# Moving the softmax reciprocals and their products at the end of a graph attention layer

## The reference, cut to what matters

```python
hl = x @ Wl.T + bl
hr = x @ Wr.T + br
s = (jnp.take(hl, src, axis=0) + jnp.take(hr, dst, axis=0)) * alpha   # alpha: edge_attr_128
s = jnp.where(s >= 0, s, SLOPE * s)                                   # leaky ReLU
smax = jax.ops.segment_max(s, dst, num_segments=n_nodes)
e = jnp.exp(s - jnp.take(smax, dst, axis=0))
denom = jax.ops.segment_sum(e, dst, num_segments=n_nodes)
att = e / jnp.take(denom, dst, axis=0)
msg = jnp.take(x, src, axis=0) * att
agg = jax.ops.segment_sum(msg, dst, num_segments=n_nodes)
out = _layernorm(x + agg, axis=-1)
```

## Time and profile before

| | |
|---|---|
| median of three runs | 1168.29 us |
| profiled execution | 1168.55 us |
| its span | 1166.5 us |
| VectorE busy | 1081.4 us (93%) |
| TensorE busy (matmul) | 1083.9 us (93%) |
| ScalarE busy | 950.3 us (81%) |
| GpSimd busy | 853.4 us (73%) |
| share of GpSimd in the chain that ended last | 55% |

### The profile page before, as it was taken

The page is one execution under the profiler, slowest core; times in us unless marked ns, Lnnn a source line. Parts: engine busy times, 40 slices in busy tenths (PEclk is TensorE's granted clock), DMA queues, the critical chain, the costliest instruction groups (busy, mean ns, idle before and its releaser), DMA issues.

```text
span 1166.5 us, 35708 instructions
## 1 busy us (share of the span) xinstructions
PE 1083.9 (93%) x9359; PEld 903.1 (77%) x9359; DVE 1081.4 (93%) x1466; ACT 950.3 (81%) x2396; POOL 853.4 (73%) x879
## 2 busy tenths in 40 slices
PE   5779999999999999999999999999999999999885
PEld 5648888888788878787887888787877878878763
DVE  6549999999999999999999999999999999999988
ACT  2548888888888888888888888888888888888895
POOL 6477777777777777777777777777777777777772
PEclk9889999999999999999999999999999999999998
DMA  8676666666666666666766666666666666666623
GB/s 221 226 218 194 187 187 189 182 193 189 180 187 185 187 183 187 185 185 186 187 184 181 186 186 184 184 186 178 187 181 183 186 188 184 184 187 185 173 64 110
DMA packets 220971, 213.49 MB, mean 183 GB/s; under 512 B 32765, under 2 KB 193796, under 8 KB 220682
## 3 DMA queue, kind: packets, MB, share of 16 engines
q0 software_dynamic: 40320, 109.96, 33.9%
q1 hardware_dynamic: 180005, 100.86, 31.2%
q10 hardware_dynamic: 461, 0.40, 0.1%
HBM read 200.39 MB, written 11.47 MB: 182 GB/s over the span
## 4 chain that ended last, share of the span: by engine, by line
POOL 55%; issue 19%; PE 15%; DVE 4%; DMA 3%; ACT 2%; SPq 1%; ACTq 0%; DVEq 0%; POOLq 0%
POOL xg L389 54%; PE ps_w L580 5%; PE ps_u L545 3%; PE ps_u L549 2%; PE ps_sT L538 2%; PE ps_z L567 1%; DVE acc L891 1%; DVE stats L962 1%; PE ps_q L561 1%; PE ps_q L589 1%; POOL attr L372 1%; DMA acc<-x_in 1%; DMA attr<-chunk_rows,chunk_at 1%; DMA line<-step_lines 1%; SPq L269 1%
## 5 line engine op out<-in xcount | busy, mean ns | idle before, releaser
L389 POOL DMA_INDIRECT xg<-gather_rows,srcT x832 | 798.8, 960 | 266.8 <-issue 252.1
L580 PE MATMUL ps_w<-onehot,ex 128*128 128x128 f32 x3328 | 407.5, 276 | 3.6 <-ACT acc L708 2.5
L580 PEld LDWEIGHTS ps_w<-onehot,ex 128*128 128x128 f32 x3328 | 389.6, 193 | 4.3 <-issue 4.3
L901 DVE TENSOR_TENSOR_SCAN ps_F<-line,B,ps_sT 128x512 f32<-128x512 bf16 x208 | 266.0, 1279 | 2.0 <-DMA line<-step_lines 1.0
L549 PEld LDWEIGHTS ps_u<-right,onehotT 128*128 128x128 bf16 x2496 | 161.8, 98 | 122.5 <-issue 120.5
L912 DVE TENSOR_TENSOR_SCAN B<-line,ps_F 128x512 f32<-128x512 bf16 x208 | 251.1, 1207 | 0.0
L545 PE MATMUL ps_u<-xg,ident 128*128 128x512 f32 x416 | 219.7, 610 | 26.8 <-DMA xg<-gather_rows,srcT 21.6
L672 ACT ACTIVATE onehotT<-ps_q,ones 128x512 bf16<-128x512 f32 x208 | 142.9, 687 | 67.0 <-PE ps_q L561 46.5
L549 PE MATMUL ps_u<-right,onehotT 128*128 x2496 | 178.2, 220 | 0.0
L925 DVE TENSOR_TENSOR ex<-ps_z,xg 128x512 f32<-128x512 f32 x208 | 142.7, 686 | 32.3 <-ACT ps_z L688 30.3
L705 ACT ACTIVATE acc<-ps_w 128x768 f32 x208 | 170.4, 819 | 0.2
(11 more groups left out here) (183 smaller groups left out, 883.7 us busy)
## 6 DMA issues: line engine op xcount, KB each, us to landing
attr<-edge_attr_in SPq DMA_DIRECT2D x832, 64.0 KB
line<-step_lines SPq DMA_DIRECT2D x208, 128.0 KB
xg<-gather_rows,srcT POOLq DMA_INDIRECT x832
gather_rows<-acc SPq DMA_DIRECT2D x12, 512.0 KB, 8.4
edge<-step_lines SPq DMA_DIRECT2D x202, 4.0 KB
acc<-x_in SPq DMA_DIRECT2D x6, 448.0 KB, 6.6
xg<-x_in SPq DMA_DIRECT2D x6, 448.0 KB, 3.8
out<-attr SPq DMA_DIRECT2D x6, 448.0 KB, 3.0
```

The source lines that it names most:

```text
L389: pool.indirect_dma_start(out=xg[:, k % SLOTS, i, :], out_offset=None, in_=rows_dram, in_offset=bass.IndirectOffsetOnAxis(ap=srcT[:, k * W ...
L580: last = nc.tensor.matmul(columns, ex[:, (k - 1) % 2, c, i, :], onehot[:, (k - 1) % 3, i, :], start=(i == 0), stop=(i == WIDE - 1), skip_g ...
L901: V.tensor_tensor_scan(ps_F[:, :], line[:, k % LINES, 0:GE], ps_sT[:, :], B[:, (k - 1) % 3, GE - 1:GE], ALU.add, ALU.max).then_inc(F_ok, 1)
```

## The change

- `RECIP` has only four entries: the reciprocals of chapters 0 to 3 stand behind the steps 198, 200, 202 and 205. That of chapter 4 stands behind the loop. Those of chapters 5 and 6 stand in ScalarE's final loop, ahead of the 1/sqrt of chapters 0 and 1.
- GpSimd waits for the last leaky ReLU (`s_ok` at 208) before the first product.
- `EARLY` is 1: the corrections of chapters 1 to 6 stand in the final stage, each behind the statistics of the chapter ahead of it.
- The output of chapters 3, 4 and 5 is written by ScalarE alone, seven blocks in place of four; VectorE's `some` is left out for them.

```diff
-    EARLY = 3
+    EARLY = 1
+
+    WHOLE = (3, 4, 5)
...
-    RECIP = [STEPS - 7, STEPS - 5, STEPS - 4, STEPS - 3, STEPS - 2, STEPS - 1, STEPS]
+    RECIP = [STEPS - 10, STEPS - 8, STEPS - 6, STEPS - 3]
...
+            pool.wait_ge(s_ok, STEPS)
             for c in range(CH):
                 cols = slice(c * CH * P, (c + 1) * CH * P)
                 pool.wait_ge(recip_ok, c + 1)
...
                 body(k)
-                for c in range(CH):
+                for c in range(len(RECIP)):
                     if RECIP[c] == k:
                         act.wait_ge(u_ps, min(k + 2, STEPS))
                         act.wait_ge(kept, k)
                         recips(c)
+            act.wait_ge(u_ps, STEPS)
+            act.wait_ge(kept, STEPS)
+            recips(len(RECIP))
             for c in range(CH):
+                if len(RECIP) + 1 + c < CH:
+                    recips(len(RECIP) + 1 + c)
                 act.wait_ge(var_ok, c + 1)
...
+                if c in WHOLE:
+                    for b in range(MOST, CH):
+                        last = nc.scalar.activation(y[:, c % 2, b, :], ps_y[c % 4][1][:, (b - QUAD) * D:(b - QUAD + 1) * D],
+                                                    ACT.Identity, bias=shift[:, c % 2, b:b + 1], scale=rstd[:, c % 2, b:b + 1])
+                    last.then_inc(yv_ok, 1)
...
-                if c >= 1:
+                if c >= 1 and c - 1 not in WHOLE:
                     some(c - 1)
```

## The result

The changed kernel takes 1174.11 us, the median of 20 runs (1172.23 to 1177.76); the kernel before took 1170.36 us beside it, also over 20 runs (1167.73 to 1176.14). The ratio is 1.0035, with a 95% interval from 1.0024 to 1.0046: slower by 4.1 us (3.75 us between the medians), less than the 0.5% that the prediction had set as the bound for "slower". The forecast time was met within 0.1 us, partly by luck: the forecast was 5.7 us above 1168.29 us, and over more runs the kernel before stands at 1170.36.

What follows compares the result with a forecast made beforehand. GpSimd's issue sets the pace up to 1101 us, then mostly VectorE in the final stage. Span 1166.5 + 5.3 + 0.4 = 1172.2, plus 2.05 around it, less 0.26 to the median: 1174.0 us, range 1164 to 1179.

Steps and rivals of the forecast that it cites:

- Leaky ReLU: Loop's end, VectorE: with no GpSimd product beside it, two stalls of 3.45 and 0.50 us go.
- Reciprocals: ScalarE, bodies 199 to 208: three early reciprocals lie nearly all in a gather's shade; last message at 1124.7, against 1132.01.
- One correction in body 208: Loop's end, VectorE: one correction, not three, so first statistics start at 1128.0, 4.6 us won.
- Products in one piece: GpSimd from 1114.4: 14 products last to about 1148.6; corrections and shifts until then can meet one.
- The lost lead: Final stage: rounds of at least 4.4 us, waits for products; with ScalarE's outputs, the end comes 5.3 us later.
- ScalarE's seven outputs: End of the final stage: 8.4 us from last correction to last output; 1.2 us are ScalarE's own.
- The clock: TensorE's products 2, 3 and 4 after waits: low clock costs between 0 and 5.1 us, taken as 0.4.
- The rival of two products for one wait: VectorE's waits up to 1143: two or three take a second product, 2.04 us each; 1178 to 1180; above 1177: 0.19.

Runs made afterwards that it cites:

- b1_nowait: The changed kernel without GpSimd's wait for the last leaky ReLU; ratio 1.0123 against the kernel before, 10 us slower than the changed kernel.
- b2_early2: The changed kernel with `EARLY` 2 in place of 1, so corrections 0 and 1 stand in body 208; ratio 1.0005 against the kernel before.
- a2_early1: The kernel before with `EARLY` 1 in place of 3, nothing else changed; ratio 1.0017, on a slower chip.
- d1_shift_psum: The changed kernel with ScalarE writing 1/sqrt a second time, to PSUM, where the shift reads it; ratio 1.0021 against the kernel before.
- g3_same_input: The changed kernel with the correction reading the message half of `acc` twice, not the denominators' half; 1806.05 us in one execution, on a slower chip.
- g4_nowhole: The changed kernel with no whole chapters on ScalarE, VectorE writing three blocks of each; ratio 1.0034 against the kernel before, on a slower chip.
- g1_best: The kernel before with GpSimd waiting for step 205's leaky ReLU, `EARLY` 2, chapters 0 to 2 whole on ScalarE, shift reading PSUM; 1794.45 us against 1797.23.

## Why the prediction was right

The mechanism was right: the loop hands over 5 us early, and the final stage loses more, for the most part for want of its lead. By steps:

1. **Leaky ReLU.** The stalls went, as forecast. What the prediction missed is how much the wait is worth beside early reciprocals: 10 us (b1_nowait), where I thought of one product or two.
2. **Reciprocals.** The exponential of step 204 came at (1107.97); forecast 1109.2, before 1111.54. A body of ScalarE without idle time takes 4.55 us (1084.77 to 1089.32 in the timeline after), a little less than the 4.65 I took, and body 199 began at (1081.76), forecast 1082.3. The five bodies give 0.7 us and the start 0.5 us of the 1.2 us by which the gain was larger. The last message came at (1123.90), forecast 1124.7.
3. **One correction in body 208.** First statistics at (1127.24), forecast 1128.0: 5.4 us won, not 4.6.
4. **Products in one piece.** End at (1147.9), forecast 1148.6. The wait for chapter 4's reciprocal was 2.63 us, forecast 1.1, and there was a second gap that I had denied: the reciprocal of chapter 6 stands behind the output of chapter 0 on ScalarE and came 1.57 us late.
5. **The lost lead.** Corrections 1 to 6 ended at (1131.4, 1138.2, 1143.9, 1149.7, 1155.6, 1160.0); forecast 1130.9, 1137.2, 1144.3, 1150.4, 1154.8, 1159.2. The shifts of chapters 0 and 1 waited (2.04 and 1.79 us). This step carries the result, though how much of it is open: with one more chapter of lead the ratio falls from 1.0035 to 1.0005, and about half of the loss is gone by the traces (b2_early2). a2_early1 has the round of 4.40 us; d1_shift_psum takes the shifts' share away, some 1.6 us by the ratio. The lead isn't the only part that lengthens the final stage: the distance grows by 4.5 us with GpSimd's wait alone, by 6.0 with the reciprocals alone, by 3.3 with `EARLY` alone, and by 7.0 with all (g3_same_input), of which 3.2 come back as the last leaky ReLU ends sooner. These overlap and don't add up.
6. **ScalarE's seven outputs.** 8.3 us from the last correction to the last output, forecast 8.4; undone, 1.1 us come back (g4_nowhole), forecast 1.2.
7. **The clock.** Mis-sized, and at another place: the products of chapters 2 and 3 had the high clock. I took 0.4 us of a possible 5.1. In the profile after it was low in half of chapter 1's products and in all of chapter 4's. It cost the statistics of chapter 1 0.7 us and those of chapter 4 1.5 us (a wait of 1.92 us, 0.42 in g3_same_input), and the distance is 2.3 us longer than in g3_same_input. Not every run has it: with 52.9 us in place of 55.1 the end would be at (1166.0), 3.7 us later than before, next to the 4.1 us of the ratio. That the median run is spared this is inferred from the sum, not shown.

Of the sum, 5.3 + 0.4 us were forecast and 4.1 us came. The sign and the step were right. The forecast was too high by what steps 2 and 3 won more, and by correction 2, which, at the high clock, waits 0.3 us and not 2.0.

The rule of "SBUF — State Buffer", section "Who interferes with whom", in the Trainium skill was borne out as to who excludes whom: with one input in PSUM the shift no longer waits. Its statement that the second to issue is blocked until the first instruction has finished holds for corrections and shifts, and not for the leaky ReLU, which waited for six (11.37 us). The rival of two products for one wait had this in the wrong place: it concerned the corrections, none of which waited for two.

## What to carry to other kernels

- If two engines exclude each other, it isn't enough to count how often they meet. Look at how many instructions the other has ready in a row: the leaky ReLU's wait of 3.45 us beside two products became 10.7 us beside six.
- To take an instruction out of a full engine is worth something only if the engine doesn't wait at that place. Here VectorE lost three outputs in chapters in which it waits for TensorE either way (0.42 us with them in g4_nowhole, 1.36 us without), while ScalarE, with them, ended 1.1 us later.
- A lead of one chapter ahead of the consumer is what keeps a chain of correction, products and statistics off the path; here it was worth more than the 2 us by which it put off the last message (b2_early2).

## What the runs showed of the hardware that wasn't expected

- **A leaky ReLU is kept out as long as GpSimd's products follow without a gap** (11.37 and 11.35 us beside six, 4.12 beside two), while every correction and every shift got in at the first boundary, also from a row of products (no correction took over 2.98 us, no shift over 2.04). All of them read twice from SBUF. That the leaky ReLU reads one tensor twice isn't reason enough, as a correction that does so got in (g3_same_input). Its neighbours on VectorE and its place among instructions that read PSUM weren't tried.
- **The same kernel took 1800 us on two other chips.** There GpSimd waits for slots, and ScalarE sits idle at places for which the trace has no releaser on this core ("remote"). Waits in the profile of g1_best: who waited for whom, us in total, times, longest.

```profile
POOL xg L391 <- DVE ex L937: 656.8, 145, 25.8
...
ACT ps_w L699 <- remote: 272.2, 83, 7.9
```

The instructions themselves are as long as elsewhere, and the final stage too. The cause is open.
